# Attention over eight batches of a graph: later batches' tokens turned by VectorE in squares and through memory

## What is computed

```python
# x: (8, 1024, 256); adj: (1024, 1024) of 0 and 1; eight heads of 32
h = jnp.maximum(_layernorm(x, axis=-1), 0.0)
q, k, v = h @ Wq + bq, h @ Wk + bk, h @ Wv + bv          # each as (b, n, 8, 32)
scores = einsum('bqhd,bkhd->bhqk', q, k) / sqrt(32)
scores = scores + (1.0 - adj)[None, None] * -1000000000.0
attn = softmax(scores, axis=-1)
out = einsum('bhqk,bkhd->bqhd', attn, v).reshape(b, n, d)
return x + out @ Wo + bo
```

## Time and profile before

| | |
|---|---|
| time, median of 3 runs (lowest to highest) | 1121.8 us (1120.91 to 1122.2) |
| the profiled execution's own time | 1119.4 us |
| its span, first to last instruction | 1117.6 us |
| busy: PE, PEld | 1096.1, 886.7 us |
| busy: ACT, DVE, POOL | 997.8, 958.5, 315.4 us |
| granted clock of TensorE, mean | 0.997 |

### The profile page before, as it was taken

The page is one execution under the profiler, slowest core; times in us unless marked ns, Lnnn a source line. Parts: engine busy times, 40 slices in busy tenths (PEclk is TensorE's granted clock), DMA queues, the critical chain, the costliest instruction groups (busy, mean ns, idle before and its releaser), DMA issues.

```text
span 1117.6 us, 28309 instructions
## 1 busy us (share of the span) xinstructions
PE 1096.1 (98%) x10672; PEld 886.7 (79%) x10672; DVE 958.5 (86%) x1796; ACT 997.8 (89%) x1835; POOL 315.4 (28%) x508
## 2 busy tenths in 40 slices
PE   8799999999999999999999999999999999999997
PEld 6677887888878888887887887888877888878775
DVE  5698988988989888998989988998988988988885
ACT  3699999998989998999999999999999999999985
POOL 6364212232214222242212412124112242112122
PEclk9899999999999999999999999999999999999999
DMA  7842352424424243332424335242352424424111
GB/s 202 253 109 50 88 147 64 105 61 111 135 72 104 64 126 101 86 102 69 130 77 116 76 81 142 68 118 75 82 141 73 103 68 101 106 65 105 51 29 49
DMA packets 88374, 109.08 MB, mean 98 GB/s; under 512 B 24752, under 2 KB 50480, under 8 KB 88240
## 3 DMA queue, kind: packets, MB, share of 16 engines
q1 hardware_dynamic: 77040, 95.89, 31.6%
q0 software_dynamic: 11008, 11.13, 5.1%
q10 hardware_dynamic: 192, 0.26, 0.1%
HBM read 30.54 MB, written 9.44 MB: 36 GB/s over the span
## 4 chain that ended last, share of the span: by engine, by line
issue 51%; DMA 30%; POOL 15%; SPq 1%; PE 1%; DVE 0%; POOLq 0%; ACT 0%; ACTq 0%; DVEq 0%
DMA inv_rows<-inv_turned 15%; DMA inv_t<-inv_rows 14%; POOL inv_t L446 10%; POOL xn L414 3%; POOL ln_t L399 1%; POOL mask L453 1%; SPq L298 1%; PE ps_scores L752 0%; POOL ln_neg_mean L396 0%; DMA q_stack<-q_lo 0%; PE ps_heads L782 0%; PE ps_side L800 0%; POOL ln_var L397 0%; POOL ln_t L403 0%; POOL ln_t L401 0%
## 5 line engine op out<-in xcount | busy, mean ns | idle before, releaser
L567 DVE CUSTOM_DVE_ANT_0 rows<-ps_scores,mask 128x1024 f32<-128x1024 f32 x512 | 615.7, 1217 | 36.4 <-PE ps_scores L733 31.1
L478 ACT ACTIVATE rows<-rows,row_min 128x1024 f32<-128x1024 f32 x512 | 589.5, 1158 | 3.6 <-DVE row_min L567 3.6
L766 PE MATMUL ps_turn<-ident_r,rows_raw 128*128 128x128 f32 x4096 | 465.6, 258 | 11.6 <-ACT turned_a L483 10.6
L766 PEld LDWEIGHTS ps_turn<-ident_r,rows_raw 128*128 128x128 f32 x4096 | 400.4, 141 | 87.0 <-ACT rows L478 29.0
L483 ACT ACTIVATE turned_a<-ps_turn 128x512 f32<-128x512 f32 x512 | 307.7, 601 | 87.1 <-PE ps_turn L766 87.0
L733 PE MATMUL ps_scores<-k_stack,q_stack 128*128 128x512 f32 x1016 | 328.7, 423 | 0.9 <-DVE row_min L567 0.9
L574 DVE COPY turned_b<-ps_turn 128x512 f32<-128x512 f32 x312 | 215.0, 689 | 85.9 <-PE ps_turn L766 80.7
L440 POOL DMA_DIRECT2D inv_rows<-inv_turned x64 | 46.6, 727 | 622.0 <-DVE inv_turned L608 616.6
L446 POOL DMA_DIRECT2D inv_t<-inv_rows x256 | 136.0, 538 | 149.1 <-DMA inv_rows<-inv_turned 144.8
L733 PEld LDWEIGHTS ps_scores<-k_stack,q_stack 128*128 128x128 f32 x1016 | 159.5, 188 | 16.9 <-DVE row_min L567 6.2
L817 PE MATMUL ps_heads<-turned_a,v 128*32 128x256 f32 x2048 | 123.8, 382 | 0.3 <-ACT turned_a L483 0.3
...
## 6 DMA issues: line engine op xcount, KB each, us to landing
...
res<-in_x SPq DMA_DIRECT2D x32, 256.0 KB, 2.8
inv_t<-inv_rows POOLq DMA_DIRECT2D x256, 32.0 KB, 2.3
out<-res SPq DMA_DIRECT2D x32, 256.0 KB, 2.8
xn<-in_x SPq DMA_DIRECT2D x30, 256.0 KB, 3.2
```

What stands on the lines that cost most here:

```text
L478: nc.scalar.activation(rows[:, k, :], rows[:, k, :], ACT.Exp, bias=row_min[:, k:k + 1], scale=-1.0, accum_out=row_sum[:, u % 2, j:j + 1]). ...
L567: nc.vector.tensor_tensor_reduce(out=rows[:, k, :], in0=ps_scores[n % 2][:], in1=mask[:, qt, :], scale=1.0, scalar=START_MIN, op0=ALU.add, ...
L766: tr = nc.tensor.transpose(ps_turn[half][:, k, :].bitcast(F32R), rows_raw[:, n % RING, kt * P:(kt + 1) * P], ident_r[:])
```

## The change

- Tokens of batches 1 to 7 are no longer turned by TensorE. VectorE transposes `xn` in 32x32 squares (`turn_squares`, four instructions of 128x512 a batch, at the slots `SQUARE_ROWS` of the first phase). GpSimd writes them to a tensor `tokens_t` in memory by two DMAs of 128 KB each (`put_squares`, eight a batch). SyncE reads them into `ht` by four DMAs of 256 KB (`ht_back`), two near the end of the first phase and two at the start of the second. A batch's tokens are loaded with eight consecutive tokens to a partition (`x_p`).
- The cut at zero moves to GpSimd. Its normalisation is two instructions a tile instead of one, done in halves of four tiles (`norm(b, half)`), half a batch earlier; the moments move to the second phase of the batch before (`STATS`).
- The last four mask tiles are converted by VectorE in slots 9, 12, 17 and 21 instead of by GpSimd.
- The inverse sums are read back by two DMAs instead of four. `INV_ROW` goes from 6 to 7 and `NORM_ROW` from 2 to 3.
- ScalarE makes 33 of a batch's 64 second copies instead of 25, VectorE 31 instead of 39.
- The orders of masks, exponentials, copies and takes within a unit are new; in the second phase `v` 0 comes ahead of `qk` 0, and in the first `o` 3 ahead of `v` 1. `store` no longer waits for its DMA; the wait and the load behind it (`reload`) come with the next step.

```diff
-MASK_AHEAD = (4, 4, 3, 3, 3, 3, 3, 3)
-EXP_AHEAD = (1, 3, 2, 2, 2, 2, 2, 1)
-EXP_AT = (0, 0, 0, 0, 0, 0, 2, 0)
-HIGH_AT = (1, 1, 0, 0, 1, 2, 0, 2)
-COPY_AT = (1, 0, 0, 1, 1, 1, 1, 1)
-TAKE_AT = (2, 1, 1, 0, 2, 2, 0, 2)
+MASK_AHEAD = (4, 3, 3, 3, 3, 4, 4, 4)
+EXP_AHEAD = (2, 2, 2, 2, 2, 2, 1, 1)
+EXP_AT = (0, 0, 0, 0, 2, 2, 1, 0)
+HIGH_AT = (2, 0, 2, 2, 1, 0, 2, 2)
+COPY_AT = (1, 1, 1, 1, 1, 1, 0, 0)
+TAKE_AT = (2, 1, 0, 1, 2, 1, 1, 0)
-INV_ROW, NORM_ROW = 6, 2
+INV_ROW, NORM_ROW = 7, 3
 STEPS = (
-    (("qk", 0, (2, 2, 3, 3)), ("qk", 1, (5, 5, 6, 6)), ("o", 2, (9, 10, 11, 11)), ("qk", 2, (13, 13, 14, 14)),
-     ("v", 0, (17, 18, 19, 19)), ("qk", 3, (21, 21, 22, 22)), ("v", 1, (25, 26, 27, 27)), ("o", 3, (28, 29, 29, 30))),
-    (("qk", 0, (1, 2, 3, 3)), ("qk", 1, (5, 5, 5, 6)), ("v", 0, (9, 10, 11, 11)), ("qk", 2, (13, 13, 14, 14)),
+    (("qk", 0, (1, 2, 3, 3)), ("qk", 1, (5, 5, 6, 6)), ("o", 2, (9, 10, 11, 11)), ("qk", 2, (13, 13, 14, 14)),
+     ("v", 0, (17, 18, 18, 19)), ("qk", 3, (21, 21, 22, 22)), ("o", 3, (25, 26, 27, 27)), ("v", 1, (29, 29, 30, 30))),
+    (("v", 0, (1, 2, 3, 3)), ("qk", 0, (5, 5, 6, 6)), ("qk", 1, (9, 10, 11, 11)), ("qk", 2, (13, 13, 14, 14)),
      ("o", 0, (17, 18, 19, 19)), ("qk", 3, (21, 21, 22, 22)), ("o", 1, (25, 26, 27, 27)), ("v", 1, (29, 29, 30, 30))),
 )
-HT_ROWS = {(0, 29): 0, (0, 30): 1, (1, 4): 2, (1, 6): 3}
-HT_UNITS = {(0, 3): 2, (1, 0): 4}
-STATS = (6, 7, 8, 15, 16, 16, 16, 23)
+STATS = (22, 22, 23, 23, 24, 26, 31, 31)
+FIRST_STATS = (8, 8, 9, 10, 11, 13, 14, 15)
+SQUARE_ROWS, FIRST_SQUARE_ROWS = (17, 17, 22, 24), (24, 25, 26, 28)
+PAIR, SQUARE_RING = 2, 3
+MASK_ROWS = (9, 12, 17, 21)
 ACT_COPIES = (
-    (2, 5, 6, 10, 13, 14, 17, 18, 21, 22, 26, 28, 29),
-    (0, 1, 2, 10, 13, 14, 18, 21, 22, 26, 29, 30),
+    (0, 3, 5, 7, 8, 11, 13, 15, 16, 17, 19, 21, 23, 24, 27, 29, 31),
+    (2, 3, 5, 7, 10, 11, 13, 15, 19, 21, 23, 24, 26, 27, 29, 31),
 )
...
+            def ht_back(b, c):
+                cols = slice(c * BANK, (c + 1) * BANK)
+                for n in range(SQUARE_RING):
+                    uses = (b * SQUARES - 1 - n) // SQUARE_RING + 1
+                    sp.wait_ge(squares_out[n], uses * PAIR * 16)
+                sp.wait_ge(qk_done, qk_step(b - 1, 1, c * CHUNKS + 1) + 1)
+                sp.wait_ge(v_done, v_step(b - 1, 1, c) + 1)
+                for k in range(DCH):
+                    sp.dma_start(ht[:, k, cols], tokens_t[k * P:(k + 1) * P, cols]).then_inc(ht_in[c], 16)
...
+                    if g == 1 and b + 1 < BATCH:
+                        ht_back(b + 1, 1)
...
-                                    sp.wait_ge(ht_turned, (b + 2) * HT_STEPS)
+                                    sp.wait_ge(squares_done, (b + 1) * SQUARES)
                                     load_x(b + 2, h)
-                        elif kind == "o":
-                            store(*((b - 1, s) if g == 0 else (b, s)))
+                        if stored:
+                            reload(*stored)
+                            stored = None
+                        if kind == "o":
+                            stored = (b - 1, s) if g == 0 else (b, s)
+                            store(*stored)
+                    if g == 0 and b + 1 < BATCH:
+                        ht_back(b + 1, 0)
...
+                for j in range(PAIR):
+                    block = pair * PAIR + j
+                    pool.dma_start(tokens_t[block * SQUARE:(block + 1) * SQUARE, :].rearrange("i (c n) -> c i n", c=PARTS),
+                                   squares[:, n % SQUARE_RING, j, :]).then_inc(squares_out[n % SQUARE_RING], 16)
...
+                for t in tiles:
+                    pool.tensor_scalar(xn[:, t, :], xn[:, t, :], ln["neg_mean"][:, t:t + 1], 0.0, ALU.add, ALU.max
+                                       ).then_inc(cut_off, 1)
...
-                for h in range(PARTS):
-                    pool.dma_start(inv_t[h * HEAD_DIM:(h + 1) * HEAD_DIM, :, :],
-                                   by_head[h].partition_broadcast(HEAD_DIM)
-                                   ).then_inc(inv_in, 16)
+                for t in range(UNIT_TILES):
+                    pool.dma_start(inv_t[:, t, :], inv_rows[t * PARTS:(t + 1) * PARTS, :].unsqueeze(1).to_broadcast(
+                        [PARTS, HEAD_DIM, P])).then_inc(inv_in, 16)
...
+                        if (b, g) == (0, 0) and u < 2:
+                            norm(1, u)
+                        elif (g, u) == (0, 0) and b + 1 < BATCH:
+                            norm(b + 1, 1)
+                        elif (g, u) == (1, UNITS - 1) and b + 2 < BATCH:
+                            norm(b + 2, 0)
+                        if g == 0 and b + 1 < BATCH:
+                            for pair in range(SQUARES):
+                                if u == (2 if b == 0 or pair >= SQUARES // 2 else 1):
+                                    put_squares(b + 1, pair)
...
+            def turn_squares(b, pair):
+                n, at = (b - 1) * SQUARES + pair, pair * PAIR * SQUARE
+                dve.wait_ge(normed, (b + 1) * TILES)
+                if n >= SQUARE_RING:
+                    dve.wait_ge(squares_out[n % SQUARE_RING], n // SQUARE_RING * PAIR * 16)
+                nc.vector.transpose(squares[:, n % SQUARE_RING].rearrange("p c (j t) -> p t c j", t=TILES),
+                                    xn[:, :, at:at + PAIR * SQUARE].rearrange("p t (c i) -> p t c i", i=SQUARE)
+                                    ).then_inc(squares_done, 1)
...
-                        pe.wait_ge(ht_done, (b + 1) * HT_STEPS + (c + 1) * DCH)
+                        pe.wait_ge(ht_in[c], (b + 1) * DCH * 16)
```

86 lines of the change are left out of this document (50 added, 36 removed).

## The result

| | before | after |
|---|---|---|
| median (lowest to highest), 5 runs each on one chip | 1121.8 us (1119.34 to 1122.77) | 1183.43 us (1181.27 to 1189.77) |
| ratio, 95% interval | | 1.0556 [1.0535, 1.0577] |
| profiled span, mean granted clock | 1117.6 us, 0.997 | 1188.0 us, 0.961 |

The account below looks back on a forecast made before the run. The prediction took TensorE's own instructions to bound the six middle batches. First batch +0.4, batches 1 to 6 -8.4, last batch +1.0 and end +1.1 made -5.9 us: 1115.9 us against 1121.8, range 1108 to 1127.

Parts of the forecast that it names:

- TensorE's term: Removing token turns saves 1.4 us in each of batches 1 to 6, leaving 132.8 to 133.1 against 134.5.
- ScalarE was hidden: ScalarE's middle-batch load rises 1.9 us to 126.2, hidden behind TensorE if the copies lie where it has room.
- the second rival: ScalarE sets the unit length, three units at 17.4 us: 1135 us; slower by ScalarE or late read-back had chance 0.17.
- The last batch: Four more ScalarE copies in its second half, with nothing covering them: +1.0 us, between 0 and 1.9.
- VectorE's moments: Moments moved to second-phase slots 22 and 23 cost nothing in the middle, covered by VectorE's 15.3 idle us a batch.
- below 0.1 us: The new step table folds one block of side work into another twice: below 0.1 us a batch either way.
- the signs of being wrong: Listed waits of TensorE for ScalarE, the DMA of `ht` or VectorE's mask rows, or a longer first-batch clock drop.
- The read-back: `ht` returns through memory, landings 2.8 and 3.2 us, before TensorE's slot 1 of the next phase: hidden, 1.8 us spare.
- VectorE's square: Each 512-element square transpose on VectorE takes 0.71 us, bounds 0.21 to 1.4; four take 2.9 us a batch.
- GpSimd: Eight more tile operations at 0.57 us; some 14 us stand ahead of the inverse sums and fit, 2 us spare.
- First batch: Turns -1.3, VectorE's load in unit 1 +1.0, lost cover in slots 25 to 28 +0.7: sum +0.4 us.
- The end: Last inverse sums turned one slot later, about 2.2 us, less two reads of 0.53: +1.1 us, between 0 and 2.

Follow-up runs that it names:

- e14: e11 with the token loads moved between the stack DMAs of `qk` 0 in the second phase: 1130.15 us, ratio to before 1.0065.
- e11: e1 with each square write cut to 32 of its 256 columns, so another output: 1133.98 us, ratio to before 1.0091.
- e2: Changed kernel with only the second phase's steps back in the order of before: 1140.52 us, ratio to before 1.0162.
- e1: Changed kernel with all four token loads issued at the start of the second phase: 1141.56 us, ratio to before 1.0158.
- e13: Kernel before plus six 128x1024 VectorE additions in slot 22 of phase 2, batches 0 to 6: 1185.46 us, ratio 1.0547.
- e4: Changed kernel with squares written without a step (another output) and GpSimd's passes as (x + a)·b, then maximum with 0: 1184.2 us, one run.
- e9: e1 with the squares in slots 16, 17, 19, 22 and three pairs written after unit 1: 1139.95 us, ratio 1.0139.
- e12: e5 with the squares of e9 and the first-batch, end and GpSimd edits of e10: 1135.24 us, ratio to before 1.0109.
- e10: e1 with `INV_ROW` 6 in the last unit, four first-batch moments and two mask tiles moved, GpSimd's form from e4: 1142.86 us.
- e5: Changed kernel with the token loads between the stack DMAs of `qk` 0 in the second phase: 1141.49 us, ratio 1.0142.
- e6: e5 with `INV_ROW` 6 instead of 7: 1148.45 us, ratio to before 1.0214.
- e7: e6 with the first-batch edits and GpSimd form of e10: 1148.45 us, ratio to before 1.0224.

## Why the prediction failed, step by step

**TensorE's term was right.** Six of eight units of a batch stand at 16.55 to 16.7 us, and two batches with hardly a wait take 132.8 and 132.9 us (e14's batch 3, e11's batch 6, both with the square writes cut) against the forecast 132.8 to 133.1. With whole writes none came below 134.0.

**ScalarE was hidden, as said.** It is busy for 126.63 and 126.10 us in the windows against the forecast 126.2, and the units that the second rival saw at 17.4 stand at 16.6. That rival did not happen. The last batch lost 0.4 of the forecast 1.0 us.

**The step that failed is VectorE's moments, "cost both at nothing in the middle; the cover is those 15.3 idle us".** It counted the moments' durations and did not follow where their input comes from, now that they stand 16 to 24 slots earlier. The load stands in SyncE's queue behind 48 issues of 0.63 us, 30 us, and the effect of the new order of steps on that queue was not costed at all: the "below 0.1 us" there was for folded blocks, judged by what TensorE does. That move of `v` 0 put the last load 4.2 us later (e2). The result was a wait of 5.8 to 8.2 us in a strictly ordered engine in each of the six batches that load tokens ahead, and the units in which they lie lost 52.1 of the 70.4 us. The prediction did list this wait among the signs of being wrong, "of `ps_scores` for the mask's row in slots 21 to 24 of the second phase (VectorE's moments)", but gave it neither price nor chance. e1, e2 and e13 settle it: taken away by either of two edits it gives back 42 or 43 of the 61.6 us, and seven holds of that kind put into the kernel before cost 63.

**Idle time was taken for cover.** VectorE's 15.3 idle us are spread in small gaps, and a single hold of 7.5 us costs 8.8 (e13). The lead of four or five rows doesn't help: the kernel has two buffers of `ps_scores`, so the scores of a row wait until VectorE has masked the row two before it. By the timelines of batch 3 of the kernel before, TensorE comes back to a buffer 0.06 to 3.9 us after VectorE has emptied it, in the median 1.2; this is the cover there is. And the price of a stall was taken as its length, while in the change thirteen stretches at half clock, 3.4 to 10.2 us long and 92 us together, stand at the stalls of TensorE; before there was one, of 6.8 us.

**Contention between transfers had no term.** The read-back was costed with undisturbed landings, 2.8 and 3.2 us. The read of `ht` did come in time, so "hidden, with 1.8 us to spare" held in its outcome, but on its way the writes delayed others' small transfers: 6.06 us for a `k_stack` piece, and 13.0 us in the fourth units of batches 1 to 6, all of which go with the bytes (e11). In the first batch's fourth unit they are worth about 2 of the 5 us (20.75 in e1, 18.66 in e11).

**VectorE's square** was right only for another form: 705 ns without the step (forecast 0.71), 1173 ns with it, inside the bounds of 0.21 to 1.4. By the Trainium skill, Vector Engine (DVE) Microarchitecture Reference, § 3.8, the transposing array keeps one element per cycle and lane; e4's 705 ns agree with the forecast's slope and the change's 1173 ns don't. By the Trainium skill, SBUF — State Buffer, § Door 1: The DMA port swizzle, each access that moves to a new 16-byte line pays; the 0.47 us between e4 and the change agree with it. In the change it did not matter for the time; in e9 and e12 a square in slot 19 did hold up a mask row.

**GpSimd** was mis-sized: 1142 and 921 ns a pass, 16.5 us a batch instead of the assumed 16 x 0.57 = 9.1, because the price of one form was taken for all. It is busy for 48 us of a batch where 39 to 43 were forecast, and e4 and e10 show that this is off the path. The 14 us that were to stand ahead of the inverse sums were also added wrongly: the terms named (read 2.1, bias 1.3, small operations 3, tile operations 4.5) make 10.9.

**First batch: +15.6 instead of +0.4.** 7.9 us of it is the same wait for `xn` in its last unit. The rest is +3.8 in unit 1, +5.0 in unit 3 and -1.1 in the others. In unit 1 stand the inverse sums, sent one place later into the crowd of the opening's transfers (e12's timeline); with `INV_ROW` 6 that unit falls from 22.49 (e5) to 19.5 (e6), while the one before grows by 1.5. The forecast's own reason, VectorE's load in unit 1, is worth 0.5 (e7) or nothing (e10). No run mended all of these two units.

**The end: +4.3 instead of +1.1.** The timeline of the last unit, against the earlier trace rows:

```profile
1172.31 0.21 DVE L676 STREAM_TRANSPOSE inv_turned<-row_inv 128x32 f32<-128x32 f32 x1
...
1177.27 1.35 POOL L502 DMA_DIRECT2D inv_t<-inv_rows  x2 [3.73 <-DMA inv_rows<-inv_turned]
...
1180.73 0.43 DVE L682 TENSOR_TENSOR heads_t<-ps_heads,inv_t 128x256 f32<-128x256 f32 x1 [7.64 <-DMA inv_t<-inv_rows]
...
1181.30 3.38 PE L877 MATMUL ps_side<-wo,heads_t 128*128 128x256 f32 x8 [3.84 <-DVE heads_t L682]
```

From the turn to the use it takes 8.4 us, before 7.2: the saving of two reads is more than lost, since the sums land beside a store (4.16 us from issue to landing, before 2.38). That is 1.3 of the 4.3. The turn itself is later, 0.3 us ahead of the first turn of the last slot where it was 1.9 ahead, which is another 1.6 (forecast 2.2). And the last eight matmuls take 3.38 us, behind a stall of 3.84 and at half clock, where they took 1.97: 1.4.

**Open:** whether a count of its own for each piece of `xn` would have saved the change's main loss without moving a load; why each stack that lands late does so (which queue or port is shared) was not looked into further; the remainder of the first batch; what the loading of eight consecutive tokens to a partition does to the transfers, which no run took back; and whether other tables would bring the 132.8 us into all batches. No version tried was faster than the kernel before.
